# A causal mask moved from GpSimd to TensorE in the last six of sixteen attention batches

## The reference, cut to what matters

```
scores = jnp.einsum('bhqd,bhkd->bhqk', q, k) / jnp.sqrt(HD)
scores = jnp.where(causal, scores, -jnp.inf)     # key <= query
attn   = jax.nn.softmax(scores, axis=-1)
ctx    = jnp.einsum('bhqk,bhkd->bhqd', attn, v)
```

## Time and profile before

| | us |
|---|---|
| three runs: median (lowest to highest) | 541.39 (540.93 to 545.23) |
| the profiled execution: its time / its span | 542.69 / 541.0 |
| busy in the span: PE / DVE / ACT / POOL | 458.8 / 324.4 / 247.3 / 203.2 |
| POOL, 128 selections of L688 | 78.6 |
| mean granted clock of TensorE | 0.938 of full |

### The profile page before, as it was taken

The page is one execution under the profiler, slowest core; times in us unless marked ns, Lnnn a source line. Parts: engine busy times, 40 slices in busy tenths (PEclk is TensorE's granted clock), DMA queues, the critical chain, the costliest instruction groups (busy, mean ns, idle before and its releaser), DMA issues.

```text
span 541.0 us, 10168 instructions
## 1 busy us (share of the span) xinstructions
PE 458.8 (85%) x3431; PEld 344.6 (64%) x3431; DVE 324.4 (60%) x974; ACT 247.3 (46%) x564; POOL 203.2 (38%) x274
## 2 busy tenths in 40 slices
PE   1668899979899999989989965787999997978874
PEld 1645667656777877767656634456999995654442
DVE  5475631135777877778868964314666664564952
ACT  1821545535555564555445522323555554434542
POOL 6620110004335435435444366870000001767761
PEclk9999999989999999999999977866999998888968
DMA  5642224644314313202357120312222201322130
GB/s 157 155 123 62 71 52 119 189 116 120 94 33 122 110 37 99 76 6 79 124 113 228 46 75 28 124 44 64 60 59 80 73 23 35 107 67 81 35 90 21
DMA packets 51441, 45.89 MB, mean 85 GB/s; under 512 B 4968, under 2 KB 46464, under 8 KB 51392
## 3 DMA queue, kind: packets, MB, share of 16 engines
q1 hardware_dynamic: 47424, 35.54, 23.4%
q0 software_dynamic: 2240, 4.53, 3.1%
q10 hardware_dynamic: 1728, 5.20, 3.0%
HBM read 26.24 MB, written 19.01 MB: 84 GB/s over the span
## 4 chain that ended last, share of the span: by engine, by line
PE 57%; POOL 16%; DVE 8%; issue 8%; DMA 5%; ACT 5%; SPq 1%; ACTq 0%; POOLq 0%; DVEq 0%
PE ps_S L1493 6%; POOL xs L741 6%; PE ps_N L1468 5%; PE ps_N L1658 5%; PE ps_P L1512 5%; POOL PT L688 4%; PE ps_N L1464 4%; PE ps_P L1668 3%; PE ps_M L1709 3%; PE ps_M L1668 3%; PE ps_S L1658 2%; PE ps_M L1555 2%; PE ps_M L1592 2%; POOL XN L750 2%; POOL LATE L750 2%
## 5 line engine op out<-in xcount | busy, mean ns | idle before, releaser
L823 ACT ACTIVATE PT<-ps_S 128x512 f32<-128x512 f32 x192 | 112.3, 591 | 109.2 <-PE ps_S L1493 87.7
L1058 DVE TENSOR_REDUCE NM<-ps_N 128x2 f32<-128x512 f32 (+1 forms) x192 | 127.9, 682 | 51.3 <-PE ps_N L1468 40.0
L688 POOL TENSOR_SCALAR_AFFINE_SELECT PT<-PT 128x512 f32<-128x512 f32 x128 | 78.6, 639 | 172.6 <-ACT PT L823 171.9
L1468 PE MATMUL ps_N<-STK 96*128 96x256 f32 (+1 forms) x256 | 105.7, 456 | 0.0
L1493 PE MATMUL ps_S<-STK 100*128 100x128 f32 (+5 forms) x352 | 88.1, 327 | 17.1 <-ACT PT L823 13.5
L1493 PEld LDWEIGHTS ps_S<-STK 104*128 104x128 f32 (+1 forms) x352 | 62.3, 200 | 25.0 <-ACT PT L823 17.9
L1464 PE MATMUL ps_N<-maskb,identb 128*128 128x256 bf16 (+1 forms) x192 | 63.5, 331 | 11.4 <-issue 8.3
L1512 PE MATMUL ps_P<-PT,VA 128*32 128x256 f32 (+1 forms) x1024 | 59.7, 351 | 7.3 <-POOL PT L688 6.8
L1468 PEld LDWEIGHTS ps_N<-STK 96*128 96x128 f32 x256 | 53.4, 208 | 4.7 <-issue 0.7
L1512 PEld LDWEIGHTS ps_P<-PT,VA 128*32 128x32 f32 x1024 | 28.1, 114 | 36.8 <-issue 15.0
L730 POOL TENSOR_TENSOR ROT<-ROT 128x256 f32<-128x256 f32 (+1 forms) x16 | 11.3, 728 | 97.1 <-DVE ROT L1087 97.1
(11 more groups left out here) (195 smaller groups left out, 811.4 us busy)
## 6 DMA issues: line engine op xcount, KB each, us to landing
STK<-scr SPq DMA_DIRECT2D x96, 96.0 KB
scr<-XQ SPq DMA_DIRECT2D x24, 256.0 KB
ROT<-in_L_ffn_W SPq DMA_DIRECT2D x16, 256.0 KB, 3.0
EW<-in_moe ACTq DMA_DIRECT2D x8, 512.0 KB, 3.6
scr<-XQ SPq DMA_DIRECT2D x24, 128.0 KB
xs<-zero SPq DMA_DIRECT2D x1, 2496.0 KB, 11.1
LATE<-xs SPq DMA_DIRECT2D x9, 256.0 KB, 2.9
ysl<-LATE SPq DMA_DIRECT2D x9, 256.0 KB, 2.3
```

The lines of the kernel that those rows point to most:

```text
L688: last = pool.affine_select(out=v, in_=v, compare_op=ALU.is_ge, fill=0.0, base=0, pattern=[[0, 4], [1, P]], channel_multiplier=-1)
L823: act.activation(PT[:, g, r, :], bank[s][:], ACT.Exp, scale=SCALE).then_inc(exp_ok, 1)
L1058: dve.tensor_reduce(NM[b % 2][:, h, qt, :].rearrange("q (p c) -> q c p", p=2)[:, slots[0]:slots[-1] + 1, :], bank[s][:].rearrange("q (c p ...
L1468: last = mm(s[:, 2 * w_ * i:2 * w_ * (i + 1)], stk[0:QK_ROWS, c, P * qt:P * (qt + 1)], stk[0:QK_ROWS, k_slots(L, c, 2 * h, 2), 0:w_], star ...
```

## The change

For the sequence numbers 10 to 15 (layer 1, batches 2 to 7) `st` opens its bank with a matmul of the mask table (stationary) and the identity (moving), which puts -1e30 where the key is later than the query, and the scores are added to it. The exponential makes zeros of these entries. The plan has no "msk" item for these batches, and `pv` waits for the third exponential of its group instead of `mask_ok`.

```diff
+PE_MASK = 10
@@ attention_plan
-            if u % 3 == 2:
+            if u % 3 == 2 and t - 2 < PE_MASK:
                 add("msk", c, u // 3)
@@ st
+                masked = seq(L, b) >= PE_MASK
+                if masked:
+                    mm(s[:].rearrange("k (h q) -> k h q", h=len(slots))[:, :, 0:P], maskb[:],
+                       identb[:, None, :].broadcast_to((P, len(slots), P)), start=True, stop=False, skip_group_check=True)
                 for i, c in list(enumerate(slots))[::m]:
                     last = mm(s[:, n * i:n * (i + m)], stk[rows, k_slots(L, c, g, 1), P * kt:P * (kt + 1)],
-                              stk[rows, c:c + m, T - n:T], start=True, stop=True)
+                              stk[rows, c:c + m, T - n:T], start=not masked, stop=True, skip_group_check=masked)
@@ pv
-                pe.wait_ge(mask_ok, 4 * n + g + 1)
+                if n < PE_MASK:
+                    pe.wait_ge(mask_ok, 4 * n + g + 1)
+                else:
+                    pe.wait_ge(exp_ok, 12 * n + 3 * (g + 1))
```

## The result

The changed kernel takes **518.35 us** (median of 4 runs, 516.22 to 522.24); the kernel before 541.97 (4 runs). The ratio is 0.956, 95% interval 0.949 to 0.963. Forecast were 538.4 and 530 to 545: the sign held, the size did not. The profiled execution took 522.24, its span is 520.2 against 541.0, a difference of 20.8. The rows call TensorE PE, VectorE DVE, ScalarE ACT and GpSimd POOL.

The account below looks back on a forecast made before the run. PE was taken to bound the kernel outside two POOL stretches. First tile -1.9, clock -1.0 and steps 14 to 17 -0.1 gave -3.0 from 542.69, so 539.7, or 538.4 on the median's scale; range 530 to 545.

Parts of the forecast that it names:

- The cap at the experts' start: Before the experts: scatters land 9.9 sooner, but PE's gate work still ends at 366.3, so only 1.9 us is gained.
- Step 13's arrival: PE from 333.91 to the gates: matmuls +2.3, rotation -2.2, one mask wait -0.2; gates reached at 353.8 again.
- The gates: PE's gate and bias work before the experts: starts at 353.8, ends at 366.3 as before, at half clock.
- the first rival: POOL's whole queue comes back, late releases go, gates run at full clock: -9.9 at the experts, about 529.5; chance 0.27.
- The first tile: Start of the experts: data there for 6 us already, so the first tile is bound by DVE, -1.9.
- The further -1.0: First expert tiles, 369 to 375: PE's clock may rise sooner without the 3.26 idle; 0 to 3 saved, 1.0 taken.
- The tail: Steps 14 to 17, after the experts: added matmuls and removed waits for POOL sum to -0.1.
- The adds: Mask matmuls in steps 14 to 17: +2.2, +1.9, +2.1 and +1.3, at 1.76 a batch at full clock, 3.5 at half.
- The returns: Steps 15 to 17: waits for POOL -0.9 and -3.5, clock -1.1, last product -1.3; rotation delay +1.4, including step 14's +2.2.
- The thing I couldn't price: Late "remote" releases of ACT and DVE during indirect DMAs: kept as they are; 0 to about 6 gained, or as much lost.
- PE's units as the longer path: Steps 14 to 17: waits for POOL return as waits for ACT, four batches pay 2.5 each; about 548, chance 0.13.
- Nothing that counts: Whole kernel: the adds eat the gain at the experts as well; 541.4, chance 0.15.

Follow-up runs that it names:

- undisturbed profile: The kernel before, unchanged, profiled a second time, with no wait "remote" in the trace; 541.24 us.
- both: The changed kernel with POOL's selections of the last six batches put back and pv waiting for them, so both mask; 541.11 us, ratio 0.997 to the kernel before.
- set 2: Runs on one chip: the change unchanged again, 520.12 us, ratio 0.961 to the kernel before at 541.24; also mask matmuls issued twice, 523.54, and tail only, 534.28.
- set 1: Runs on one chip of four variants of the change, with selections or mask matmuls kept, removed or replaced, beside the kernel before at 541.91 us.
- no mask: The changed kernel without its 72 mask matmuls, so the last six batches are unmasked; 517.73 us, ratio 0.959 to the kernel before.
- the other condition: Sets with many waits "remote"; the unchanged changed kernel, run again in set 4, took 565.54 us there, ratio 1.045 to the kernel before.
- the tiny operation: The changed kernel with a two-column POOL operation in place of each removed mask, same waits, pv waiting for it; 525.04 us, and 543.52 in a later set.

## Why the prediction was wrong, by its own steps

**The cap at the experts' start is the step that failed.** It said that POOL's landing comes 9.9 sooner but PE's gate work would still end at 366.3. The landing was right: 9.7 behind the first scatter. The cap was not: PE's gate work ended at 351.5, and the first tile waited for the landing. The failure has three terms.
- *Step 13's arrival* was charged +2.3 for matmuls and credited -0.2 for "one short wait for a mask". From the first unit after the rotation to the gates PE took 19.9 before and 14.7 after: -5.2, not +2.1. The wait for the mask is 4.11 in the undisturbed profile (3.50 in "both"), and the stretch is 14.6 as soon as nobody waits for masks, even with the selections still in POOL's queue (334.02 to 348.65). The rotation came 3.7 sooner, the forecast 2.2 and the 1.5 from before the stretch. This term alone lifts the cap: from 344.9 on, gates of the old length would have ended at 357.4, still ahead of the rows at 358.05.
- *The gates* were taken at their old length of 12.5. They took 6.6, at full clock. That the idle ahead of them, which went with the mask, had set their clock is argued: after 4.11 of idle they ran at half clock throughout, after 3.50 in "both" from their middle on. I had them at half clock in the forecast and at full clock only in the first rival.
- *The first tile* was therefore bound by the landing: -11.5 and not -1.9. The further -1.0, for a clock that rises sooner in the first tiles, gave nothing: PE idled longer than before (6.57, not 3.26), and from the first tile to step 14 took 80.3 in both. The time ahead of the experts is the first rival's, chance 0.27, whose 529.5 erred mainly in what it gave the tail. Its reason was in part luck: it had the late releases go with the masks, and the second profile of the kernel before has all its masks and no late release.

**The tail, forecast -0.1, gave -9.2 (-9.9 in set 2).** The adds were charged about 7.5 in all and cost 3.4 to 3.9 by single traces (removed once, doubled once); why not more is argued, not shown: some fall where PE waits, and some may raise the clock share. The returns were put at 7.6 and are about 13. By step, second profile of before against after: step 14 nothing (forecast +2.2); from the start of step 15 to its first output transposes 10.9 to 7.5, -3.4 (forecast -0.8 with the +2.2 passed on), the rotation above; from those of step 16 to those of step 17 -3.8 (forecast -2.5, for step 16 with its clock); step 17 -2.1 (forecast 0).

**The thing I couldn't price lay behind both.** I kept the late releases "as they are, since the DMAs stay". They belong to a condition in which that one profile was taken: there are none in the second profile of before, at the same time of 541. In it PE and DVE were late in just the places where POOL was late too, and where two things are late at once the trace names one; so POOL's lag looked like 0.2 and 0.8 where alone it was 4.1 and 3.2. The kernel before takes 541 either way; POOL's queue, not PE, seems to set its pace. The bounds given, 0 to 6 gained or "as much lost", were far too narrow: the loss can be 45 us (565.5 against 520).

**The clock.** In set 1 the mean granted clock over the runs is 0.927 in the kernel before (13 runs) and 0.939 in "both" (10 runs). At 1 minus the clock, over one half, times the span, that is 78 and 66 us at half clock: the added matmuls went with 12 us less of it, which may be how they come to cost so little. This agrees with the rule weighed, of the Trainium skill's "TensorE: Matmul & The Clock Gate", Part 1, that activity releases the throttled clock. The other pair does not settle it: "no mask" has 0.950, the change 0.960 in the result but 0.950 again in set 2, so 52 us at half clock against 41 or 52.

**The other rivals.** PE's units as the longer path (548): no. The waits for ACT that it foresaw in place of those for POOL come to 2.6 in the tail. Its sign came true in the other condition, by another mechanism. "Nothing that counts": no. The prices of a mask matmul held: in the chain of the changed kernel its pieces at full clock are 0.12 to 0.13 us for 256 columns and 0.22 to 0.24 for 512 (0.11 and 0.22 were charged), and its load of weights, 0.10, overlaps the matmul.

**What stays open.** Why PE stalls beside indirect DMAs issued back to back in some sets and not in others was not found; in the traces ACT and DVE are released late, and PE's matmuls start late with no wait named. Whether it is the chip or its state at the time isn't told apart: each set had one chip, two and the result's without the stalls and three with; the profile that the prediction read has late releases as well, and a time like any other. No kernel was found that wins in both conditions: the tiny operation is 525.0 in one and 543.5 in the other, the change 518 to 520 and 565.5.

## What to carry to other kernels

Before a step is declared covered by another engine's work, ask whether that work's own lateness is caused by the step; take a second profile if the first has waits with no named releaser, since two late engines hide each other. An item in a queue costs its time even when nobody waits for it. An engine that idles ahead of dense work can pay twice, by the wait and by a half clock after it. Items that break up a burst of DMAs can be worth more than they cost: measure a kernel that loses them on more than one chip.

## What the runs showed of the hardware

- With 20 scatters or 22 gathers issued back to back, each about 0.96 us and 0.30 between them, PE can stall: idle stretches of 5.78, 5.38 and 8.40 us marked "issue", exponentials released up to 9.4 us late, 33 matmuls in 20 us instead of 115. In other sets the same instructions show none of it.
- In a set with late releases, kernels whose series is broken up by selections or by waits for ACT of about 3 us took 539.5 and 543.5, against 541.6 for the kernel before; that is 7.1 and 18.5 us more than they took in a set without, where the change lost 45.
- 72 masking matmuls cost -0.8 (on the kernel) to 3.9 us (in the tail of a trace); in one pair of kernels 12 us of half clock went with them, in another 0 to 11.
- An idle of 4.11 us ahead of the gates left them at half clock, 11.5 us; one of 3.50 let them start at full clock, 8.6 us; with 0.47 ahead of them they took 6.6.
